# Attention's bias matmuls first in their banks, the scores last, and the second pair of row blocks behind the value products

## The reference, cut to what matters

```
bias   = tisa_bias(offsets, amplitudes, sharpness, l)   # depends on i - j only, one row per head
logits = einsum('bhld,bhmd->bhlm', q, k) * scale + bias[None]
attn   = softmax(logits, axis=-1)
out    = einsum('bhlm,bhmd->bhld', attn, v)
```

## Time and profile before

| | us |
|---|---|
| median of 3 runs | 1184.66 (1184.16 to 1185.03) |
| the profiled execution, its own time | 1184.06 |
| its span in the trace | 1182.1 |
| first exponential of the attention loop, start | 83.04 |
| attention loop ends, about | 500 |
| TensorE busy over the span | 1020.0 |
| VectorE busy over the span | 983.5 |
| ScalarE busy over the span | 719.0 |

### The profile page before, as it was taken

One profiled execution on the slowest core, in us unless ns is written; L12 is line 12 of the kernel. 1 busy time (PEld: TensorE's weight loads), 2 busy tenths in 40 slices (PEclk: granted clock), 3 DMA queues, 4 the chain that ended last, 5 costly groups with the idle time before them and its releaser, 6 DMA issues. The chain is left out here.

```text
span 1182.1 us, 19693 instructions
## 1 busy us (share of the span) xinstructions
PE 1020.0 (86%) x5756; PEld 540.9 (46%) x5756; DVE 983.5 (83%) x2432; ACT 719.0 (61%) x1175; POOL 447.7 (38%) x404
## 2 busy tenths in 40 slices
PE   3559999999999999785999999782877769999998
PEld 1212222222222222264766676541656537666775
DVE  6589999889999986168999999787876689999997
ACT  5116665666666656564777777586333537777775
POOL 4600000000000000013777778515663127777776
PEclk9659999999999999967999999986889879999999
DMA  3740122032012200000000000000000000000001
GB/s 100 255 95 8 61 76 49 16 106 66 15 55 75 57 1 2 1 21 12 20 21 18 22 18 23 3 19 0 1 0 0 21 9 21 22 18 21 19 23 38
DMA packets 56704, 41.66 MB, mean 35 GB/s; under 512 B 23334, under 2 KB 51004, under 8 KB 56636
## 3 DMA queue, kind: packets, MB, share of 16 engines
q1 hardware_dynamic: 54268, 38.18, 12.0%
q10 hardware_dynamic: 2368, 2.63, 0.8%
HBM read 33.12 MB, written 7.47 MB: 34 GB/s over the span
## 5 line engine op out<-in xcount | busy, mean ns | idle before, releaser
L514 POOL TENSOR_TENSOR f_act_low<-f_act,f_act_high 128x512 fp32r<-128x512 f32 x256 | 331.2, 1294 | 151.3 <-ACT f_act_high L471 146.3
L1203 ACT ACTIVATE at_prob<-at_cols 128x1024 f32<-128x1024 f32 x256 | 248.1, 1021 | 198.4 <-PE at_cols L1092 198.4
L1255 DVE CUSTOM_DVE_ANT_0 at_rows<-at_rows,at_table_max 128x512 f32<-128x512 f32 x512 | 340.3, 719 | 33.5 <-PE at_rows L1057 32.3
L471 ACT CAST f_act_high<-f_act 128x512 fp32r<-128x512 f32 x256 | 159.1, 621 | 68.1 <-DVE f_act L591 65.7
L585 DVE TENSOR_TENSOR f_gated<-f_relu,f_work 128x512 f32<-128x512 f32 x256 | 174.3, 681 | 21.3 <-PE f_work L417 15.1
L591 DVE TENSOR_TENSOR f_act<-f_gated,f_work 128x512 f32<-128x512 f32 x256 | 175.8, 687 | 10.2
L478 ACT ACTIVATE f_relu<-f_work 128x512 f32<-128x512 f32 x256 | 152.9, 597 | 32.1 <-PE f_work L362 30.7
L360 PE MATMUL f_work<-f_x_high,f_wu_high 128*128 128x512 f32 x256 | 148.4, 580 | 2.7 <-DVE f_wu_low L573 2.1
L1057 PE MATMUL at_rows<-at_k_stack,at_q_stack 48*128 48x512 bf16 x512 | 104.7, 405 | 39.9 <-DVE at_maxima L1255 38.4
L1104 PE MATMUL at_pv<-at_prob,at_v_stack 128*32 128x512 f32 x1024 | 136.4, 605 | 0.6 <-ACT at_prob L1203 0.6
L1092 PE MATMUL at_cols<-at_table_cols,flip_sum 128*64 128x512 f16 x1024 | 136.4, 387 | 0.0
(11 more groups left out here) (274 smaller groups left out, 1393.8 us busy)
## 6 DMA issues: line engine op xcount, KB each, us to landing
at_table_cols<-bias_rows SPq DMA_DIRECT2D x32, 248.0 KB, 5.1
at_table_max<-bias_rows SPq DMA_DIRECT2D x12, 480.0 KB, 4.3
f_wu<-in_L_ffn_up_w_dram SPq DMA_DIRECT2D x64, 64.0 KB, 2.0
f_wd<-in_L_ffn_down_w_dram SPq DMA_DIRECT2D x64, 64.0 KB, 1.8
at_q_stack<-q_parts SPq DMA_DIRECT2D x28, 96.0 KB, 2.4
at_k_stack<-k_parts SPq DMA_DIRECT2D x24, 96.0 KB, 3.9
at_table_max<-bias_rows ACTq DMA_DIRECT2D x4, 480.0 KB, 5.8
k_parts<-at_parts SPq DMA_DIRECT2D x2, 768.0 KB, 5.4
```

The costliest lines, as they stand in the source:

```text
L471: nc.scalar.copy(act_h[:, j % 4, :], act[:, j % 4, :]).then_inc(act_high, 1)
L514: nc.gpsimd.tensor_tensor(act_l[:, k, :], act[:, k, :], act_h[:, k, :].bitcast(F32), ALU.subtract).then_inc(act_low, 1)
L1203: act(prob[:, S % 2, 2 * hp:2 * hp + 2, :], s2[:, hp, :, :], ACT.Exp).then_inc(exp_done, 1)
L1255: nc.vector.tensor_tensor_reduce(out=slot, in0=slot, in1=t_max[:, 2 * p.hp + j, c:c + BANK][:, ::-1], scale=1.0, scalar=-3.0e38, op0=ALU.a ...
```

## The change

In step S, the bias matmuls go first and open the banks (`start=True`), and the wait for the exponential of step S - 1 goes with them. The wait for the tables' chunks goes along. The scores come after the first pair of row blocks, close the banks (`stop=True`) and raise `cols_ready`. The products of step S - 1 go ahead of the second pair of row blocks, which becomes the last thing in a step. No instruction is added or removed; SP's, ScalarE's, VectorE's and GpSimd's queues are not edited.

```diff
                 def scores(S, hp):
                     it, s = S // STEPS, S % STEPS
                     b, lh, mb = it % BATCH, s // LT, LT - 1 - s % LT
+                    for j in range(2):
+                        r = slice(HALF * j, HALF * j + QK_ROWS + PIECES)
+                        last = mm(s2[:, hp, j, :], k_st[r, b, hp, mb * P:(mb + 1) * P],
+                                  q_st[r, b, lh, hp, :], start=False, stop=True)
+                    last.then_inc(cols_ready, 1)
+
+                def biases(S, hp):
                     if S > 0:
                         pe.wait_ge(exp_done, 2 * (S - 1) + hp + 1)
                     for j in range(2):
-                        r = slice(HALF * j, HALF * j + QK_ROWS + PIECES)
-                        mm(s2[:, hp, j, :], k_st[r, b, hp, mb * P:(mb + 1) * P],
-                           q_st[r, b, lh, hp, :], start=True, stop=False)
-
-                def biases(S, hp):
-                    for j in range(2):
                         for u in range(2):
                             c = step_columns(S % STEPS, u)
-                            last = mm(s2[u * HALF:(u + 1) * HALF, hp, j, :], m.flip_sum[:],
-                                      t_col[:, 2 * hp + j, c:c + BANK], start=False, stop=True)
-                    last.then_inc(cols_ready, 1)
+                            mm(s2[u * HALF:(u + 1) * HALF, hp, j, :], m.flip_sum[:],
+                               t_col[:, 2 * hp + j, c:c + BANK], start=True, stop=False)
...
                     if phase_out_in(S) is not None:
                         turn_outputs(phase_out_in(S))
+                    if it % BATCH == 0:
+                        for c in range(CHUNKS):
+                            if chunk_starts[c] == s:
+                                pe.wait_ge(tab_in[c], 32 * (it // BATCH + 1))
+                    for hp in range(2):
+                        biases(S, hp)
                     for n in pairs[:1]:
                         rows_pair(n)
                     if s % LT == 0:
...
                         scores(S, hp)
                     if phase_turned_in(S) is not None:
                         turn_maxima(phase_turned_in(S))
-                    if it % BATCH == 0:
-                        for c in range(CHUNKS):
-                            if chunk_starts[c] == s:
-                                pe.wait_ge(tab_in[c], 32 * (it // BATCH + 1))
-                    for hp in range(2):
-                        biases(S, hp)
+                    if S > 0:
+                        products(S - 1)
                     for n in pairs[1:]:
                         rows_pair(n)
-                    if S > 0:
-                        products(S - 1)
```

## The result

The changed kernel takes 1190.68 us (median of 7 runs, 1189.34 to 1191.80), the kernel before 1184.66: a ratio of 1.0046, 95% interval 1.0035 to 1.0057. It is slower by 6.0 us; 1191.4 was forecast. The profiled execution took 1191.25, with a span of 1189.3, 7.2 over that of before.

The account below looks back on a forecast made before the run. TensorE's 3.06 us step barely bounded the kernel; ScalarE's chain would now set 3.20. Ordinary steps +9.9, late steps -2.4, start -0.8 sum to +6.7 on 1184.06, and 0.6 for the median gives 1191.4 us, range 1185.5 to 1197.

Parts of the forecast that it names:

- ordinary steps: Loop steps of the usual kind: 71 intervals, each 0.14 us longer (3.20 for 3.06), +9.9 us in all.
- TensorE's own work: TensorE's loop per step: same 20 matmuls and four changes of shape, so 3.06 us, unchanged.
- The chain: Last exponential to next step's first: signal 0.06, biases 0.54, first pair 0.23, scores and signal 0.43; 1.26 for 1.12 us.
- The unknown that I bounded by 0.1 either way: Bias matmuls starting just after a wait, weights not loaded: step 3.10 to 3.30, 7 us either way over 71.
- The late steps: Steps where VectorE is late for a pair: 3.68 for 3.84 us, about -0.15 each, 16 of them, -2.4 us.
- The transposes: Steps with outputs' or maxima's transposes, 14 each: 3.65 and 3.20 us, nothing gained or lost.
- The start: Loop's beginning: biases run in TensorE's idle time, first exponential 0.5 us earlier, second interval 0.3 shorter.
- The signs to look for: ScalarE idle 1.26, TensorE idle 0.1 to 0.2 before biases and less busy, intervals 3.20, 3.68, 3.65, VectorE's L1255 wait up.
- case 2: Rival: TensorE stays the bound, steps 3.06 to 3.08, only the start gains; 1183.9, up to 1185.5 us; chance 0.12.
- (3): Rival: VectorE's lateness is hidden, the 16 intervals of 3.84 fall to 3.06, -12.5; 1171.4 us; chance 0.05.
- (4): Rival: the first pair's slot binds inside the chain, a step costs 3.30; 1198.5 us; chance 0.10.
- (5): Rival: TensorE's pauses lower the clock; a tenth of steps at 1.2 GHz, 13 losing 2.5 us each; 1224; chance 0.03.

Follow-up runs that it names:

- e1_pair_ahead: Against the changed kernel: first pair moved ahead of the biases, second pair ahead of the products, banks still opened by biases; 1185.83 us, 1.0004 of the kernel before.
- e2_pair_behind: Against the changed kernel: first pair moved behind the scores, second left behind the products; 1192.99 us, 1.0074 of the kernel before.
- e5_pair_placed: Against the changed kernel: first pair behind the scores except in the maxima's step, outputs' transposes behind the biases; 1182.99 us, 0.9979 of the kernel before.
- e6: Against the changed kernel: half 1's scores ahead of half 0's, both signalled together, one more matmul pass in the chain; 1206.91 us, 1.0177 of the kernel before.
- e3: Against the kernel before: only the products and second pair swapped, scores still opening the banks; 1277.70 us, 1.0785 of the kernel before.
- e7: The changed kernel run and profiled a second time, no edit; 1190.44 us, 1.0039 of the kernel before.
- e4: Against the changed kernel: second pair put back ahead of the products; 1238.25 us, 1.0452 of the kernel before.

## Why the prediction was right, and where it was off

**The total: closer than its parts.** Between the two profiled executions +6.7 was forecast and +7.2 measured. By the forecast's own terms: ordinary steps +9.8 for +9.9, late ones -3.1 for -2.4, the maxima's +0.7 for 0, the start +0.4 for -0.8, and behind the loop -0.5 for 0. The mechanism and its main term were right. That the sum is within 0.5 is in part luck: the start and the maxima's steps came out 1.9 too high, the late steps and the stages behind the loop 1.2 too low.

**TensorE's own work unchanged, 3.06: right.** e1_pair_ahead and the ordinary steps of e2_pair_behind and e5_pair_placed run at 3.06 with the banks opened by the biases. The changes of shape, four in each order, cost the same in sum, as the forecast took from the 0.09 of the earlier trace rows. The drain at a change of mode that the Trainium skill states (TensorEngine Tiling (Array Packing), "Key Properties") agrees with these rows and was neutral, as its count is the same.

**The chain, 1.26: right to the hundredth.** The rows show 1.26 of idle time and 3.20, and each link within 0.01 of its term. That it is this chain, and the pair in it, is shown from both sides: without the pair 3.06 (e1, e2), with 0.22 more 3.41 (e6). The unknown that I bounded by 0.1 either way, bias matmuls that start right after a wait, cost nothing to be seen (0.60 from the exponential's end to the pair, as reckoned).

**The late steps, -0.15 each: right in the main.** 3.68 was forecast and is measured; -2.5 in 14 and -0.6 in two more, for -2.4 in all. The 3.84 of the earlier trace rows was a short one of its kind, whose mean is 3.87, and the two in the last head group gained 0.32 each and not 0.15. e6_half0_last shows the mechanism: the longer ScalarE's chain, the more of VectorE's lateness it covers.

**The transposes, 0: nearly.** Outputs' 3.65 as said; maxima's 3.24 for 3.20, +0.7 where I had 0.

**The start, -0.8: wrong, though small.** The first exponential did come 0.5 earlier. But the next two intervals were 4.06 and 3.56 where I had 3.20 each, so the start lost 0.4 instead of gaining 0.8 (the 0.14 that each interval from the second on was to cost is counted with the ordinary steps). I took the full clock for granted from step 1 on. The busy time in the stretch from 84 to 88 us shows otherwise (columns as above). The kernel before:

```profile
84.00:88.00 4.00, 3.14 (x26) 0.83 (x24) 3.40 (x11) 2.43 (x4) 0.00 (x0) 1.00 0.00 0
```

The changed kernel:

```profile
84.00:88.00 4.00, 4.00 (x22) 0.68 (x18) 2.39 (x8) 1.87 (x3) 0.00 (x0) 0.56 0.00 0
```

The granted clock was 1.00 and is 0.56, that is at its lower level (1.2 GHz) for most of the stretch, and TensorE's timeline shows it in the biases of step 1, against those of step 2:

```profile
83.61 1.98 PE L1093 MATMUL at_cols<-at_table_cols,flip_sum 128*64 128x512 f16 x8
...
88.52 1.05 PE L1093 MATMUL at_cols<-at_table_cols,flip_sum 128*64 128x512 f16 x8
```

It rose some 3 us later, and in the nine traces the time of the rise goes with TensorE's order in step 0:

| kernels | order in step 0, behind the pairs taken ahead | granted clock, 84 to 88 us | first two intervals, us |
|---|---|---|---|
| before; e3 | pair, scores, biases | 1.00; 1.00 | 3.51, 3.05; 3.38, 3.99 |
| e2; e5 | biases, scores, pair | 1.00; 1.00 | 3.31, 3.05; 3.41, 3.05 |
| the change; e7; e4 | biases, pair, scores | 0.56; 0.54; 0.57 | 4.06, 3.56; 4.06, 3.62; 4.07, 3.55 |
| e6 | biases, pair, scores (half 1 first) | 0.66 | 4.48, 3.42 |
| e1 | pair, biases, scores | 0.50 | 4.71, 3.51 |

(An ordinary step is 3.98 in e3, 3.55 in e4 and 3.41 in e6.) No order occurs with both an early and a late rise, so chance is an unlikely cause. It isn't the early biases by themselves, as e2 and e5 show. What in the order delays the rise stays open: no run varies step 0 alone.

**The signs to look for.** ScalarE's idle time, its cause and the intervals came as written (the scores' line is L1083 in the changed kernel). VectorE's wait before L1255 rose, but little, from 32.3 to 36.7 us in all. TensorE's 0.1 to 0.2 of idle time before the biases does not stand in its matmul rows; the wait on L1203 is found at their weight loads (0.43 above). "TensorE is busy less of the stretch" did not come: 344.57 us for 341.42. A matmul's row is 0.38 long and the next starts 0.22 behind it, so a pause of 0.14 between two starts leaves no hole in the busy time; it removes overlap. The same holds for the idle time that was looked for. The count of matmuls started in the stretch fell by 1.9%, and that was the right thing to name.

**The rivals.** That TensorE stays the bound (case 2) is refuted by 3.20; that the lateness is hidden (3) holds for 0.18 to 0.32 of some 0.8 and does not pay for the rest; that the slot binds inside the chain (4) does not occur in an ordinary step, the pair follows the biases without a wait, 1.44 behind the pair before it (310.18 to 311.62), where e3 and e4 show that a slot comes free in 1.24 to 1.25; the clock (5) stayed at 1.00 in the loop and mattered only at its start.

## What to carry to other kernels

When two loops through different engines have nearly the same period (here 3.06 through TensorE and 2.98 through ScalarE), a reordering that leaves each engine's work alone can still cost its whole difference in step time: list what stands, in queue order, between the end of the last consumer and the start of the next, and add it up. Work that only fills time (the row pairs) belongs outside that list, but it has a spacing of its own, given by how soon its buffers come free, so two edits that are each ruinous alone can be harmless together. Judge an order by each kind of step and not by the ordinary one: e2_pair_behind had an ordinary step 0.14 shorter than the change's, and no better time.

## What the runs showed of the hardware that was not expected

A change of matmul shape costs about the same from row pairs to bias matmuls (0.32 start to start, 310.18 to 310.50 in the change) as from row pairs to products (0.32), against 0.22 to 0.23 between equal shapes, and whether a bank is opened by the one or the other kind makes no difference to an ordinary step (e1_pair_ahead, 3.06). The clock's rise at the loop's start differs by some us between kernels that differ only in the order of their first steps (granted clock from 84 to 88 us 1.00 before and in e5_pair_placed, 0.56 in the change); the first two intervals are longer than those of before by 1.1 us in the change and by 1.7 in e1_pair_ahead. And equal total times can hide opposite errors: e3_products_only and e4_banks_only both came within 1 us of their forecasts with ordinary steps 0.09 shorter than reckoned, and the one with outputs' steps, the other with maxima's steps, 0.56 longer.
